# Two-layer decoder on one core: three groups of steps stand elsewhere in the order of TensorE, VectorE and GpSimd

## What is computed

```python
# sublayer 2: mLSTM-like memory attention to a context (8 heads of 16)
C = (qk + k_hop) * D;  h = C / (normalizer + eps) @ v;  hn = norm per head(h)
x = _layernorm(x + hn * (1 + w) + b)
# sublayer 3, first half: norm, then causal attention with rope (16 heads of 8)
h = layernorm(x) * g + b;  x = x + softmax(mask(rope(q) @ rope(k).T)) @ v @ Wproj
# sublayer 4: causal attention with rope; sublayer 5: attention to the context with a bias
x = _layernorm(x + attn(x));  x = _layernorm(x + xattn(x, ctx, fside, mask))
# sublayer 6: 16 experts, top 2
h = gelu(_layernorm(x @ W1[e] + b1[e]));  out = h @ W2[e] + b2[e]
```

## Time and profile before

| | before |
|---|---|
| median of 3 runs | 4112.23 us |
| the profiled execution's own time | 4112.38 us |
| its span in the profile | 4110.4 us |
| TensorE busy / weight loads | 2877.3 us (70%) / 1936.0 us (47%) |
| VectorE busy | 2394.2 us (58%) |
| ScalarE busy | 1599.7 us (39%) |
| GpSimd busy | 1858.3 us (45%) |
| mean granted TensorE clock | 0.869 of full speed |

### The profile page before, as it was taken

One profiled execution on the slowest core, in us unless ns is written; L12 is line 12 of the kernel. 1 busy time (PEld: TensorE's weight loads), 2 busy tenths in 40 slices (PEclk: granted clock), 3 DMA queues, 4 the chain that ended last, 5 costly groups with the idle time before them and its releaser, 6 DMA issues.

```text
span 4110.4 us, 92550 instructions
## 1 busy us (share of the span) xinstructions
PE 2877.3 (70%) x27760; PEld 1936.0 (47%) x27761; DVE 2394.2 (58%) x6956; ACT 1599.7 (39%) x3994; POOL 1858.3 (45%) x2306
## 2 busy tenths in 40 slices
PE   3999999758888888884048878888988840266600
PEld 2666666435555555552036646656666530155500
DVE  2777777427777777875001147777777770144455
ACT  2666666324444444441013335555555520011100
POOL 4222222016665656663730036666666616511177
PEclk9999999978998989986579989999999975599955
DMA  2111111441111111110222211111011102211133
GB/s 54 39 38 40 40 40 43 144 136 42 46 47 41 47 40 47 46 35 25 77 71 74 68 38 29 28 29 27 27 29 28 27 10 67 65 54 56 55 82 87
DMA packets 282376, 207.13 MB, mean 50 GB/s; under 512 B 61730, under 2 KB 246455, under 8 KB 281904
## 3 DMA queue, kind: packets, MB, share of 16 engines
q1 hardware_dynamic: 262960, 164.88, 13.6%
q0 software_dynamic: 19200, 39.62, 3.5%
HBM read 114.99 MB, written 90.18 MB: 50 GB/s over the span
## 4 chain that ended last, share of the span: by engine, by line
issue 22%; POOL 13%; PE 12%; DVE 4%; POOLq 1%; DMA 0%; ACT 0%; DVEq 0%; ACTq 0%; SPq 0%
PE scores_ps L1047 3%; POOL rows L2051 2%; POOL k_bd L1999 2%; POOL got L2096 2%; POOL shared L2149 2%; POOL shared L1999 2%; POOL norm_rstd L1995 1%; PE desk_ps L1054 1%; PE heads_ps L1054 1%; PE scores_ps L1163 1%; PE scores_ps L1165 1%; PE desk_ps L1163 1%; PE heads_ps L1163 1%; DVE shared L1904 1%; DVE e_T L1817 1%
## 5 line engine op out<-in xcount | busy, mean ns | idle before, releaser
L1995 POOL TENSOR_TENSOR norm_rstd<-norm_veps,minus_half 128x1 f32<-128x1 f32 x384 | 211.8, 552 | 483.3 <-DVE norm_veps L1553 483.3
L2051 POOL DMA_INDIRECT rows<-e_in,slot_put x256 | 249.0, 973 | 163.9 <-issue 107.4
L1278 ACT ACTIVATE turned<-scores_ps 128x512 f32<-128x512 f32 x384 | 227.8, 593 | 165.9 <-PE scores_ps L905 159.7
L1571 DVE TENSOR_REDUCE row_max<-scores_ps 128x8 f32<-128x512 f32 x384 | 262.2, 683 | 32.0 <-issue 16.0
L1274 ACT ACTIVATE probs<-probs 128x512 f32<-128x512 f32 x384 | 240.6, 627 | 89.9 <-DVE probs L1573 89.5
L1573 DVE TENSOR_TENSOR probs<-scores_ps,row_max 128x512 f32<-128x512 f32 x384 | 265.4, 691 | 13.3
L905 PE MATMUL scores_ps<-consts,probs 128*128 128x128 f32 x1536 | 247.6, 285 | 13.8 <-ACT probs L1274 12.9
L1206 ACT ACTIVATE probs<-probs 128x512 f32<-128x512 f32 x256 | 161.3, 630 | 136.1 <-DVE probs L1492 133.7
L1490 DVE TENSOR_REDUCE row_max<-scores_ps 128x8 f32<-128x512 f32 x256 | 174.7, 682 | 63.0 <-PE scores_ps L756 58.1
L905 PEld LDWEIGHTS scores_ps<-consts,probs 128*128 128x128 f32 x1536 | 178.8, 145 | 24.4 <-ACT probs L1274 18.5
L1904 DVE COPY shared<-turned_ps 128x256 f32<-128x256 f32 x72 | 30.5, 424 | 263.5 <-PE turned_ps L1155 263.5
(11 more groups left out here) (338 smaller groups left out, 8336.4 us busy)
## 6 DMA issues: line engine op xcount, KB each, us to landing
hop_dram<-shared SPq DMA_DIRECT2D x64, 256.0 KB, 2.1
hop_in<-hop_dram SPq DMA_DIRECT2D x64, 256.0 KB, 2.9
rows<-zero_rows SPq DMA_DIRECT2D x64, 144.0 KB, 1.9
shared<-rows SPq DMA_DIRECT2D x72, 128.0 KB, 2.1
moe<-shared SPq DMA_DIRECT2D x72, 128.0 KB, 1.9
rows<-zero_rows SPq DMA_DIRECT2D x64, 128.0 KB, 1.8
c_in<-in_ctx SPq DMA_DIRECT2D x128, 64.0 KB, 1.9
c_two<-in_ctx SPq DMA_DIRECT2D x128, 64.0 KB, 2.2
```

Of the source, the lines that this page charges most:

```text
L1278: act.activation(turned[a][:, 512 * g:512 * g + 512], scores_ps[:, a, g, :], ACT.Identity)\
L1571: dve.tensor_reduce(best, sc, AX, ALU.max).then_inc(at.shift.sem, 1)
L1995: pool.tensor_tensor(n_rstd[:, k, u, :], n_veps[:, k, u, :], minus_half[:, 0:1], ALU.pow).then_inc(sig.sem, 1)
L2051: pool.indirect_dma_start(out=rows, out_offset=bass.IndirectOffsetOnAxis(ap=slot_put[:, c, U * n + i:U * n + i + 1], axis=0), in_=put_rows ...
```

## The change

No operation is added, removed or resized. On TensorE: in the third stage the transpose of `xn` stands ahead of the memory scores; in the fifth the causal mask of attention 0 stands right behind its weighing, and the transpose of `x4` behind the logits and keys; in the second experts the second layer stands last in a pair. On VectorE, third stage: the gates' sum goes behind the second norm's statistics, and the application of the causal attention's norm goes ahead of the product with the decay. On GpSimd, fifth stage: the spread of attention 1's keys goes from the middle to just before the other spread.

```diff
 # TensorE, third stage
+                if live(i):
+                    after(pe, mixed.of(i), f_logits_copied.of(i - 4), f_v_copied.of(i - 1))
+                    pe.transpose(desk_ps[:, 0:P], xn[u], ident).then_inc(xn_turned.sem, 1)
                 if live(i + 2):
                     after(pe, m_copied.of(i + 1), m_shift.of(i + 1), ...)
...
                     last.then_inc(m_scored.sem, 1)
-                if live(i):
-                    after(pe, mixed.of(i), f_logits_copied.of(i - 4), f_v_copied.of(i - 1))
-                    pe.transpose(desk_ps[:, 0:P], xn[u], ident).then_inc(xn_turned.sem, 1)
 # TensorE, fifth stage
                     weigh5(a5[0], 0, v_bd[1 - u])
-                if live(i + 3):
-                    after(pe, norms[0].of(i + 3), rotated.of(i + 2))
-                    pe.transpose(heads_ps[:, 0:P], x4[(j + 3) % UN], ident).then_inc(x4_turned.sem, 1)
+                if live(i + 2):
+                    after(pe, a5[0].copied.of(i + 1))
+                    causal5(0)
...
+                if live(i + 3):
+                    after(pe, norms[0].of(i + 3), rotated.of(i + 2))
+                    pe.transpose(heads_ps[:, 0:P], x4[(j + 3) % UN], ident).then_inc(x4_turned.sem, 1)
                 if live(i):
                     turn5(a5[1], 1, i, 0)
-                if live(i + 2):
-                    after(pe, a5[0].copied.of(i + 1))
-                    causal5(0)
 # TensorE, second experts
-                if live_pair(i - 1):
-                    layer(i - 1, 1 - w, (heads_ps, desk_ps)[1 - w], o_g_T[1 - w], o_w2, o_b2, ...)
                 if live_pair(i + 2):
                     turn_slots(i + 2, w)
...
                     last.then_inc(s["o_hturned"], 1)
+                if live_pair(i - 1):
+                    layer(i - 1, 1 - w, (heads_ps, desk_ps)[1 - w], o_g_T[1 - w], o_w2, o_b2, ...)
 # VectorE, third stage: the order of the steps behind the cmax sum
-  gates' sum (i+7); norm_heads, z sum, stats5 (i); product with decay (i+1);
-  apply5 x_out (i-3); apply5 x2, stats5 (i)
+  norm_heads, z sum, stats5 (i); apply5 x_out (i-3); product with decay (i+1);
+  apply5 x2, stats5 (i); gates' sum (i+7)
 # GpSimd, fifth stage
                 if live(i + 1):
-                    after(pool, b_k_copied.of(i + 1), a5[1].score.of(i - 1))
-                    spread5(k_ring[2 + 1 - u], b_k[1 - u], "head16").then_inc(b_spread.sem, 1)
                     after(pool, norms[1].of(i + 1, norms[1].per - 1))
                     rstd5(norm_rstd[1], 1, 1 - u)
...
+                if live(i + 1):
+                    after(pool, b_k_copied.of(i + 1), a5[1].score.of(i - 1))
+                    spread5(k_ring[2 + 1 - u], b_k[1 - u], "head16").then_inc(b_spread.sem, 1)
                 if live(i + 3):
                     after(pool, rope_added.of(i + 3))
                     spread5(k_ring[1 - u], rope_k[1 - u], "head16").then_inc(a_spread.sem, 1)
```

More of the change, by code:

```diff
@@ L1174, in period @@
                           ((s["o_T_done"], i + 4), (s["o_hn_done"], i + 2)), s["o_up"])
-                if live_pair(i - 1):
-                    layer(i - 1, 1 - w, (heads_ps, desk_ps)[1 - w], o_g_T[1 - w], o_w2, o_b2,
-                          ((s["o_g_done"], i + 2), (s["o_out_done"], i)), s["o_down"])
                 if live_pair(i + 2):
@@ L1184, in period @@
                     last.then_inc(s["o_hturned"], 1)
+                if live_pair(i - 1):
+                    layer(i - 1, 1 - w, (heads_ps, desk_ps)[1 - w], o_g_T[1 - w], o_w2, o_b2,
+                          ((s["o_g_done"], i + 2), (s["o_out_done"], i)), s["o_down"])
             pair_periods(pe, period)
@@ L1666, in period @@
                        .then_inc(m_shift.sem, 1)
-                if live(i + 7):
-                    after(dve, gates_ready.of(i + 7), block_done.of(i + 4) if j4 == 1 else gated.of(i + 6))
-                    dve.tensor_tensor(gates4[:, 16 * ((j + 7) % 4):16 * ((j + 7) % 4) + 16], mix_ps[:, 0:16], g_row[:], ALU.add)\
-                       .then_inc(gated.sem, 1)
                 if live(i):
@@ L1675, in period @@
                     stats5(mixed, 11, 0, i, u, z[u])
+                if live(i - 3):
+                    apply5(f_norm, 2, 1 - u, x_out[1 - u], y[1 - u], f_rstd.of(i - 3), h_turned.of(i - 5),
+                           (xn_stored[1 - u], 16 * (i - 3 - (1 - u)) + 32))
                 if live(i + 1):
@@ L1679, in period @@
                                       decay[1 - u].rearrange("p (g n) -> p g n", g=NR), ALU.mult).then_inc(m_shift.sem, 1)
-                if live(i - 3):
-                    apply5(f_norm, 2, 1 - u, x_out[1 - u], y[1 - u], f_rstd.of(i - 3), h_turned.of(i - 5),
-                           (xn_stored[1 - u], 16 * (i - 3 - (1 - u)) + 32))
                 if live(i):
@@ L1686, in period @@
                     stats5(mixed, 15, 1, i, u, x2_ring[j4])
+                if live(i + 7):
+                    after(dve, gates_ready.of(i + 7), block_done.of(i + 4) if j4 == 1 else gated.of(i + 6))
+                    dve.tensor_tensor(gates4[:, 16 * ((j + 7) % 4):16 * ((j + 7) % 4) + 16], mix_ps[:, 0:16], g_row[:], ALU.add)\
+                       .then_inc(gated.sem, 1)
                 if j4 == 0 and live(i + 4):
```

## The result

The changed kernel takes 4054.77 us (median of 4 runs, 4047.58 to 4061.27); the kernel before, beside it, 4114.76 (4104.75 to 4129.95). The ratio is 0.9865, interval 0.9842 to 0.9888: 60 us faster, where 159 were forecast. 4054.77 lies above the range (3905 to 4010). The profiled execution took 4058.4 us, with a span of 4056.3, 54 less than before.

The account below looks back on a forecast made before the run. The prediction took a chain of waits between engines, with no engine always busy, to bound the kernel. Its terms 52 + 72 + 0 + 27 + 8 = 159 us, off 4112, gave 3953 us, range 3905 to 4010.

Parts of the forecast that it names:

- The step that failed: Fifth stage, GpSimd: the moved spread costs nothing, ending 1.2 us before the scores of attention 1 read it.
- the term of 72 us: Fifth stage: TensorE's wait for `x4` goes, 1.15 us in each of 63 periods; bounds 50 and 76.
- 8 of the clock: Fifth stage: 8 us gained from less time lost at half clock; bounds 0 and 17.
- three signs of being wrong: L1002 waiting for VectorE, attention 1's scores waiting for the spread, or the third stage's granted clock below 0.90.
- Rival 2: Fifth stage: VectorE takes over, `x4` stays late and half of that gain goes, 3989 us; chance 0.08.
- the 0.6 that I had counted: Fifth stage: `x4` comes about 0.6 us earlier against L1076 once the power has no spread in front.
- The third stage: 52 us: Waits at L936 and L905 go by moving the `xn` transpose, 0.82 us in each of 63 periods; bounds 35 and 62.
- The clock of the third stage: 27 us: Less standing still cuts the third stage's half-clock loss from 76 to 49 us; bounds 76 gained and 76 lost.
- The 76 us: Third stage before the change: half clock costs 1.21 us in each of 63 periods, 76 us.
- The line through two stages: Clock loss against standing still, drawn through third and fifth stages; the third's loss falls from 0.10 to 0.065.
- rival 1: Whole kernel: the waits go but the clock returns nothing, 3988 us; chance 0.14.
- The second experts: 0: Moving the second layer last in a pair gains 0 us; bounds a gain of 71 and a loss of 14.

Follow-up runs that it names:

- Experiment 3: Changed kernel with TensorE's fifth stage back in its old order, GpSimd's two spreads still side by side: 4118.31 us, 1.002 of before.
- experiment 5: Changed kernel with the spread of attention 0's keys on GpSimd moved to right behind the power for `x4`, apart from the other spread: 3958.73 us, 0.9638 of before.
- experiments 2: Changed kernel with only GpSimd's spread of attention 1's keys back in its old place, TensorE's new order kept: 4045.65 us, 0.9846 of before.
- experiment 9: Changed kernel with GpSimd's two spreads apart and TensorE's fifth stage in its old order: 3995.84 us, 0.9718 of before.
- experiment 7: Changed kernel with TensorE's third stage in its old order, VectorE's new list kept: 4104.25 us, 0.9987 of before.
- experiment 6: Changed kernel with VectorE's third stage in its old order, TensorE's moved transpose of `xn` kept: 4047.94 us, 0.9850 of before.

## Why the prediction was wrong

**The step that failed** is in the fifth stage: "The moved spread costs nothing as long as it ends before the scores of attention 1 read it." I asked of the moved spread only who reads it. That part held: no product waits for it. I didn't ask what it pushes. The other spread, now behind it, runs beside VectorE's copy and holds it for 1.66 us per period, so `x4` stays late and the term of 72 us (and 8 of the clock) measured a loss of 7.5. Of the three signs of being wrong that I named, none came; I had none for a longer instruction. Experiment 3 prices the edit at 72 us alone; with TensorE's part beside it, the stage takes 88 us more than when the spreads are apart (experiment 5). Rival 2 named VectorE as the engine that might take over, with a chance of 0.08 and half the price. Its argument against, that VectorE's "two waits in a period" are more than what is taken out, counted VectorE's work as fixed.

The trace of before had a sign of it. The application of `x5` takes 0.48 us at 2719.63 against 0.35 for the same instruction on `x4`; from 2719.57 GpSimd runs a product with both operands in SBUF. In the changed kernel it starts before that product (at 2620.97, the product at 2621.14) and takes 0.34. I copied both durations and didn't ask for the difference.

**The rest of the fifth stage was right**, as experiments 2, 5 and 9 show. `x4` is late because of the power behind the spread: with the power freed and nothing held, its wait goes from 1.01 to 0.39 us (experiment 9), the 0.6 that I had counted. Mask and keys fill what is left. TensorE's edit alone gives nothing, GpSimd's order without the hold gives 49 us, and both together 81. With the hold away the period is 12.83 us, where 13.97 - 1.15 = 12.82 was counted, and the granted clock is 1.00:

```profile
2380.00:3160.00 780.00, 745.24 (x8626) 518.17 (x8624) 668.05 (x1871) 463.01 (x1273) 545.20 (x719) 1.00 0.12 30
```

**The third stage: 52 us** were counted at full clock, and 13.98 - 13.09 = 0.89 us per period, or 56, came; with the periods of 13.33 it is slightly less (13.97 to 13.10 on average, 55). The waits of L936 and of L905 went as said.

**The clock of the third stage: 27 us** is shown by no run, and its base was misread. The 76 us were all that lies above the full-clock period, and I called all of it half clock. They hold the four stands at L936 by "issue", 10.7 us; the changed kernel's 69 us hold five, 15.1. The prediction had read the waits of one period only, at most 0.77 us. In before, the clock is at 1.2 GHz within 2 us after each of the four stands of 1.83 to 3.15 us. That much agrees with the rule that the prediction cites from the Trainium skill ("TensorE: Matmul & The Clock Gate", Part 1), that the clock falls after an idle stretch. But it also falls at 1477, in a period whose longest wait is 0.77 us, and of such falls that rule says nothing. As for the size: the eight traces of the changed third stage took 879.6 to 894.2 us, on average 887.1; less 63 x 13.09 that is 62 us above full clock, which against 76 would be a gain of 14. But experiment 7, with TensorE's order and period of before, has 939.2 - 63 x 13.98 = 58, and against that there is no gain. With one trace of before and one of experiment 7 not even the sign can be told. The line through two stages is refuted as little as it is confirmed; rival 1, by which the clock returns nothing, is as near.

**The second experts: 0** was right (346.9 and 347.0 us). Had the label with VectorE been the reason for the 0.98 us, some of it would have gone; so "issue" was the better label. That it is the reading of the two numbers is argued from the code, and no run tests it.

**The sum.** Of the 54 us in the profiled executions the third stage gives 62.7, the way to it and from it to the fifth 7.6, the fifth takes 7.5, and the end behind the experts, which nothing touches, took 203.2 us instead of 194.5. In the nine experiments it took 198.2 to 206.3, so 8 us of it is spread between executions; why the one trace of before lies below them all isn't known. A time near the forecast can be had: experiment 5 with its one moved spread measures 3958.73 against the forecast of 3953, 149 us under the kernel before beside it, of 159. That it comes so near is in part luck: its profiled execution has one of the shorter third stages of the eight, 880.9 us.

Open is what starts a stretch of half clock in the third stage, what the stands by "issue" at L936 are, and where in the chain the 0.3 us of experiment 6 arise.

## What to carry to other kernels

When an instruction moves, look at what it pushes and at what then runs beside it on the other engines, not only at who reads its result. For GpSimd's long operations in SBUF this means: list what VectorE does in those microseconds, put copies and anything with two operands in SBUF elsewhere, and let reductions and reads of PSUM run beside them. An instruction whose duration in the trace is far above its usual one and ends where another engine's ends is a hidden wait; the views of idle time don't show it, but the min/median/max of a line do. And before a stage's excess over its best period is called the clock's, look through all its periods for waits that one period doesn't show.

## What the runs showed of the hardware

- A copy of 128x2 f32 from SBUF to SBUF takes 0.16 us alone and 1.82 us when a 128x1024 product on GpSimd (1.89 us, both operands in SBUF) has started 0.11 us before it. A `tensor_reduce` of the same data takes 0.14 us there. A `scalar_tensor_tensor` with two 128x128 operands in SBUF goes from 0.35 to 1.60 us (median over the trace 1.76).
- VectorE's operations on PSUM aren't slowed: in the stretch of the fifth stage the row maximum takes 685 ns and the product 691 on average after, and 684 and 691 before; the two beside the first spread above take 0.68 and 0.69 us.
- The spreads themselves take 1.89 to 1.92 us on average in every kernel, beside a held copy or not: here the engine that came first loses nothing.
- In the third stage of the eleven traces the granted clock falls to 1.2 GHz within 4 us of 40 of the 54 stands of 1.8 to 3.9 us at L936, and it falls also in periods whose longest wait is 0.77 us; in the fifth stage of experiment 5, whose longest wait in a usual period is 0.24 us, it is 1.00 on average, which is 2.4 GHz.
